# Rounding x for the last four row tiles on ScalarE: one step moved, and every engine's order written anew

## The reference, cut to what matters

```python
x = x + xattn(layernorm(x), ctx, ctx, mask, ...)      # 16 heads of 32; scores -> mask -> softmax -> v -> @ wo + bo
x = x + ffn(layernorm(x), w1, b1, w2, b2)

def act_quant(x):                                      # per row, to whole numbers from -127 to 127
    scale = 127.0 / clip(max(abs(x)), 1e-05)
    return clip(round(x * scale), -128, 127) / scale
def weight_quant(w):                                   # per matrix, to -1, 0, 1
    scale = 1.0 / clip(mean(abs(w)), 1e-05)
    return clip(round(w * scale), -1, 1) / scale
def bitlinear(x, w, b):
    return act_quant(rmsnorm(x)) @ weight_quant(w).T + b
h = gelu(bitlinear(x, w1, b1))                         # 512 -> 2048
return bitlinear(h, w2, b2)                            # 2048 -> 512
```

## Time and profile before

| | |
|---|---|
| median of 3 runs | 652.19 us (651.63 to 652.81) |
| the profiled execution | 650.6 us, span 648.8 us |
| granted TensorE clock | 1.000 in the mean, in every slice of the page |
| busy: PE / DVE / ACT / POOL | 628.9 / 574.3 / 530.2 / 518.7 us |
| share of the chain that ended last | PE 67%, POOL 13%, DVE 8%, DMA 4%, ACT 4%, issue 3% |

### The profile page before, as it was taken

One profiled execution on the slowest core, in us unless ns is written; L12 is line 12 of the kernel. 1 busy time (PEld: TensorE's weight loads), 2 busy tenths in 40 slices (PEclk: granted clock), 3 DMA queues, 4 the chain that ended last, 5 costly groups with the idle time before them and its releaser, 6 DMA issues.

```text
span 648.8 us, 14114 instructions
## 1 busy us (share of the span) xinstructions
PE 628.9 (97%) x4904; PEld 423.7 (65%) x4904; DVE 574.3 (89%) x1062; ACT 530.2 (82%) x1450; POOL 518.7 (80%) x653
## 2 busy tenths in 40 slices
PE   8988999999999999999999999999999999999996
PEld 6746886666666676766666676666667666565542
DVE  5697889999999988999899988999889799999894
ACT  2579679987889888887898878888988889998674
POOL 3297977979977898688967899778959778999776
PEclk9999999999999999999999999999999999999999
DMA  8983310424315443354224343043333122543236
GB/s 291 402 300 111 126 41 9 107 45 106 84 28 115 103 91 75 38 135 90 71 67 114 74 121 74 10 132 87 90 74 74 24 75 41 128 86 88 62 61 182
DMA packets 109286, 65.38 MB, mean 101 GB/s; under 512 B 90856, under 2 KB 90856, under 8 KB 108576
## 3 DMA queue, kind: packets, MB, share of 16 engines
q1 hardware_dynamic: 108159, 64.49, 37.9%
q10 hardware_dynamic: 1056, 0.00, 0.1%
HBM read 35.12 MB, written 8.39 MB: 67 GB/s over the span
## 4 chain that ended last, share of the span: by engine, by line
PE 67%; POOL 13%; DVE 8%; DMA 4%; ACT 4%; issue 3%; SPq 0%; POOLq 0%; DVEq 0%; ACTq 0%
PE ps_a L573 23%; PE ps_y L710 11%; PE ps_z L687 11%; PE ps_t L646 6%; PE ps_s L636 4%; PE ps_a L658 3%; POOL hid L2270 2%; POOL prob L2259 2%; DMA q_hT<-q_h 2%; PE ps_y L580 2%; DVE hs L1633 2%; POOL q_h L2275 2%; PE ps_a L607 2%; ACT prob L1145 2%; DMA wk_s<-in_L_xattn_wk_dram 1%
## 5 line engine op out<-in xcount | busy, mean ns | idle before, releaser
L1145 ACT ACTIVATE prob<-ps_s,nmax 128x120 f32<-128x120 f32 x512 | 178.9, 377 | 24.7 <-DVE nmax L1579 19.2
L2259 POOL TENSOR_TENSOR prob<-prob,pinv 128x480 f32<-128x480 f32 x128 | 129.2, 1017 | 41.0 <-DVE pinv L1584 40.0
L687 PE MATMUL ps_z<-w1T,q_xT 128*128 128x512 fp8e4 x476 | 122.8, 380 | 0.5 <-DVE hid L1625 0.4
L1145 ACT ACTIVATION_READ_ACCUMULATOR prob<-ps_s,nmax 128x1 f32 x512 | 113.3, 221 | 0.0
L710 PE MATMUL ps_y<-w2T,q_hT 128*128 128x512 fp8e4 x448 | 105.5, 379 | 1.5 <-DMA q_hT<-q_h 1.5
L1625 DVE SCALAR_TENSOR_TENSOR hid<-ps_z,y_deq,b_row 128x512 f32<-128x512 f32 x119 | 88.0, 739 | 10.6 <-PE ps_z L687 9.2
L1576 DVE COPY_PREDICATED_SCALAR ps_s<-hidden_key,masked_c 128x480 f32 x128 | 90.5, 707 | 4.2 <-PE ps_s L636 3.9
L1121 ACT COPY probT<-ps_t 120x512 f32<-120x512 f32 x128 | 76.9, 601 | 15.4 <-PE ps_t L646 14.3
L1579 DVE TENSOR_REDUCE nmax<-ps_s 128x4 f32<-128x480 f32 x128 | 84.1, 657 | 4.4
L646 PE MATMUL ps_t<-ident,prob 128*120 128x128 f32 x512 | 77.9, 275 | 4.3 <-POOL prob L2259 3.7
L646 PEld LDWEIGHTS ps_t<-ident,prob 128*120 128x120 f32 x512 | 60.0, 137 | 25.3 <-issue 7.4
(11 more groups left out here) (207 smaller groups left out, 1373.7 us busy)
## 6 DMA issues: line engine op xcount, KB each, us to landing
x<-in_x_dram SPq DMA_DIRECT2D x32, 256.0 KB, 2.9
out_dram<-x SPq DMA_DIRECT2D x32, 256.0 KB, 2.8
xn<-in_x_dram SPq DMA_DIRECT2D x7, 1024.0 KB, 6.6
hid<-in_L_ffn_w_dram SPq DMA_DIRECT2D x4, 1024.0 KB, 9.6
ctx_k<-in_ctx_dram SPq DMA_DIRECT2D x8, 240.0 KB, 3.1
ctx_k<-in_mask_Bx1xSxS_ik_dram SPq DMA_DIRECT2D x7, 240.0 KB, 3.1
xn<-in_x_dram SPq DMA_DIRECT2D x4, 256.0 KB, 3.5
x<-in_L_xattn_wq_dram SPq DMA_DIRECT2D x1, 1024.0 KB, 7.3
```

What stands on the lines that cost most here:

```text
L687: last = nc.tensor.matmul(bank[:], q_xT[:, k % 3, i], w1T[:, i, c * CH:(c + 1) * CH], start=(i == 0), stop=(i == KD - 1))
L1145: last = nc.scalar.activation(prob[:, n % 3, g * S2:(g + 1) * S2], ps_s[n % HG][:, g * S2:(g + 1) * S2], ACT.Exp, bias=nmax[:, n % 4, g:g ...
L2259: gp.tensor_tensor(pr, pr, pinv[:, n % 4].unsqueeze(2).to_broadcast([P, HG, S2]), ALU.mult).then_inc(s["prob_ready"], 1)
```

## The change

Two things change. For the row tiles 28 to 31 `round_x` on GpSimd ends after its first step, and a new `round_x` on ScalarE takes MAGIC off and writes q_x. And all five lists are written in another order; apart from the four new calls they hold the same calls as before. The parts of the diff that the prediction speaks of, from the lists with the unchanged lines left out:

```diff
+        XLATE = NT - 4
 # SP
-            load_piece(1)
-            load_piece(0)
-            load_piece(3)
-            load_piece(2)
+            load_piece(2)
+            load_piece(0)
+            load_piece(1)
+            load_piece(3)
...
 # TensorE, head
             turn_xn(0, 2)
+            turn_xn(0, 3)
             project_ctx(0, "k")
-            turn_xn(0, 3)
+            first_q(0)
             turn_keys(0)
-            first_q(0)
...
             turn_xn(1, 0)
-            turn_piece(3, (0, 1))
             turn_probs(2)
-            turn_piece(3, (2, 3))
+            turn_piece(3, (0, 1))
             turn_probs(3)
+            turn_piece(3, (2, 3))
             total_weights(1)
...
 # ScalarE
+            def round_x(k):
+
+                act.wait_ge(s["y_magic"], k + 1)
+                act.wait_ge(s[f"qxT{(k - 2) % 3}_in"], 16 * ((k - 2) // 3 + 1))
+                nc.scalar.activation(q_x[:, k % 2], yw[:, k % 2], ACT.Copy, bias=-MAGIC).then_inc(s["qx_ready"], 1)
+
...
 # VectorE, head: scale_bq() moves from before sum_abs(3) to behind weight_scales(0)
 # VectorE, tile 26
-            evac_up(27, 1)
             h_scale(26)
-            invert_sums(123)
             oT_low(29)
+            invert_sums(123)
             softmax_max(124)
...
 # GpSimd
             def round_x(k):
                 gp.tensor_scalar(yw[:, k % 2], yw[:, k % 2], yq[:, 2, t:t + 1], MAGIC, ALU.mult, ALU.add
                                  ).then_inc(s["y_magic"], 1)
+                if k >= XLATE:
+                    return
                 pool.wait_ge(s["y_magic"], k + 1)
...
             round_x(28)
             normalize(123)
+            add_bo(29)
             round_h(26)
             normalize(124)
-            add_b2(27)
+            add_b2(26)
             normalize(125)
...
 # GpSimd, before normalize(112): h_factor(23) and add_b2(25) move behind it
```

More of the change, by code:

```diff
@@ L451, in _ @@
             turn_x(3)
+            turn_h(1)
             load_mask(2)
-            turn_h(1)
+            turn_x(4)
             load_ctx(3)
@@ L878, in _ @@
             project_q(2, 2)
+            turn_probs(26)
+            ffn_up(3, 3)
             turn_ctx(3)
-            ffn_up(3, 3)
-            turn_probs(26)
             project_out(5)
@@ L1516, in _ @@
             gelu(29)
+            round_x(31)
             square_h(29)
@@ L2366, in _ @@
             y_factor(1)
-            add_bo(2)
-            normalize(15)
+            normalize(17)
             add_b2(1)
-            normalize(16)
-            normalize(17)
-            add_bo(3)
+            round_x(2)
+            normalize(18)
             add_bo(4)
-            round_x(2)
-            add_bo(5)
-            normalize(18)
-            y_factor(2)
-            normalize(19)
-            normalize(20)
-            round_h(0)
-            h_factor(0)
+            normalize(19)
@@ L2382, in _ @@
+            round_h(0)
+            normalize(20)
+            y_factor(2)
+            h_factor(0)
+            add_bo(5)
             add_b2(2)
-            y_factor(3)
             normalize(21)
             round_x(3)
+            y_factor(3)
+            add_b2(3)
             normalize(22)
-            add_b2(3)
             round_h(1)
             ln1_factors(3, 0, 4, 12)
+            ln1_apply((0, 1))
             normalize(23)
             normalize(24)
-            ln1_apply((0, 1))
             h_factor(1)
+            normalize(25)
@@ L2394, in _ @@
+            add_b2(4)
             round_x(4)
-            normalize(25)
+            ln1_apply((2, 3))
+            normalize(26)
             round_h(2)
-            normalize(26)
-            ln1_apply((2, 3))
+            normalize(27)
             y_factor(4)
-            normalize(27)
-            add_bo(6)
             normalize(28)
             h_factor(2)
+            add_bo(6)
             normalize(29)
             round_h(3)
-            add_b2(4)
             for a in range(2, 6):
+                round_x(4 * a - 3)
@@ L2409, in _ @@
                 y_factor(4 * a - 3)
-                round_x(4 * a - 3)
                 normalize(16 * a - 2)
+                normalize(16 * a - 1)
+                normalize(16 * a)
                 add_bo(4 * a - 1)
                 h_factor(4 * a - 5)
-                add_b2(4 * a - 3)
-                normalize(16 * a - 1)
-                normalize(16 * a)
                 round_x(4 * a - 2)
                 normalize(16 * a + 1)
+                round_h(4 * a - 4)
                 normalize(16 * a + 2)
+                h_factor(4 * a - 4)
@@ L2420, in _ @@
                 normalize(16 * a + 3)
+                normalize(16 * a + 4)
+                add_b2(4 * a - 3)
+                y_factor(4 * a - 2)
                 add_bo(4 * a)
-                round_h(4 * a - 4)
-                y_factor(4 * a - 2)
-                normalize(16 * a + 4)
                 normalize(16 * a + 5)
+                round_x(4 * a - 1)
+                normalize(16 * a + 6)
+                y_factor(4 * a - 1)
+                round_h(4 * a - 3)
+                normalize(16 * a + 7)
@@ L2437, in _ @@
-                ln1_factors(a + 2, 0, 4, 3 * a + 9)
-                normalize(16 * a + 10)
-                round_h(4 * a - 2)
                 add_b2(4 * a)
```

800 lines of the change are left out of this document (401 added, 399 removed).

## The result

| | before | after |
|---|---|---|
| median | 651.33 us (20 runs: 650.31 to 652.81, and one at 908.49) | 654.38 us (20 runs, 652.12 to 658.01) |
| ratio | | 1.0045, 95% interval 1.0032 to 1.0058 |
| profiled execution | 650.6, span 648.8 | 655.14, span 653.3 |

Slower by 0.45%, some 2.9 us, and with more scatter: eight of the twenty runs lie between 652.1 and 652.9, the other twelve between 653.1 and 658.0. I had 652.3 and 0.48 on no change; it came out on the side to which I gave 0.27, 0.08 above the end of my range (654.3, which was 2.1 above the median of before; measured are 3.05 above the median of twenty).

What follows compares the result with a forecast made beforehand. TensorE's own work bounds the loop, four engines bind one another from 535 to 603 us, and tile 29's q_h fixes the end. +1.05 - 0.60 - 0.39 + 0.1 = +0.16 on the 652.19 median: 652.3 us, range 650.3 to 654.3.

Steps and rivals of the forecast that it cites:

- rival 2: Head loss paid in full, nothing absorbed, through ScalarE's evacuations of weight piece 3: +1.75, 653.95 us; chance 0.22.
- The head, +1.05: Before the loop: later weight sum, GpSimd's and ScalarE's new orders delay the second weight-sum product; +1.05, bounds 0.25 and 1.65.
- my own point (57.1): In the head: a second line-719 product starting later than 57.1 us decides for the rival of a fully paid head.
- gave back 0.60: Late TensorE finds its awaited normalize ready at 102 us: 0.60 taken back, bounds 0 and 1.85.
- The middle: From 103 to 535 us: 0 for the loop itself, bound +1.8 for four passes of one wait.
- 535 to 603 us, -0.39 and +0.1: Normalize(112) freed of work ahead, -0.39; tile 26's q_h later through add_bo(29), +0.1, bounds -1.6 and +0.5.
- The moved step, 0 (bounds -0.3 to +0.6): Late tiles 28 to 31: four q_x roundings go from GpSimd to ScalarE as 0.60-us copies, hidden or without gain; 0.
- The tail, 0 (bounds -0.5 to +0.8): After 603 us: VectorE has the same work up to h_scale(29), so tile 29's q_h arrives as before; 0.
- Rival 1: End is won: GpSimd relieved, TensorE's waits of 0.38, 0.68 and 1.03 go; -1.64, 650.55 us; chance 0.20.
- Rival 3: Table changes: a switch takes 2.66 instead of 1.28, ScalarE late at 140 us; +2.8, 655.2 us; chance 0.03.
- Rival 4: round_x on GpSimd was covered anyway; all difference comes from the orders; no chance of its own.
- The signs: Profile after: line-719 products near 27.1 and 57.0, tile 26's wait under 1.6, last long wait for tile 29's q_h.

Runs made afterwards that it cites:

- a1: Kernel before with the five head lists of the kernel after, loops, tails and moved step as before: 1.0002, 651.55 us.
- a3: Kernel before with the loop lists of the kernel after, heads and tails as before: 1.0003 (0.9994 to 1.0012).
- a2: Kernel before with the five tail lists of the kernel after and the moved step, heads and loops as before: 1.0053, 654.72 us.
- b2: Kernel before with the tail lists of the kernel after, but round_x's second step kept on GpSimd for all tiles: 1.0041, 653.72 us.
- c1: Kernel after with GpSimd's add_bo(29) moved back behind normalize(120), no longer ahead of round_h(26): 1.0045, ten runs from 652.04 to 658.90 us.
- d2: Kernel after with SP's load_residual(28) moved behind turn_x(26), ahead of turn_h(24): 1.0022, 652.39 us.
- c2: Kernel after with VectorE's subtraction of the mean in the summing form for tile 30 alone: 1.0034, 653.29 us.
- a4: Kernel after with VectorE's subtraction of the mean in the summing form for all tiles: 1.0076, 656.52 us.
- b1: Kernel before, all its lists, with only round_x's second step of tiles 28 to 31 moved to ScalarE: 1.0073, 655.82 us.

## Why the prediction missed, step by step

The span of the profile after is 4.53 us longer than that of before. By the lags 0.2 of this were there at 454 us, where I had +0.45; 1.75 more came by gelu(27), where I had -0.29; 2.2 more up to the last half gelu and 0.4 behind it, where I had 0. So the steps that failed are the stretch from 535 to 603 us and the tail. That the median still lies close to the end of the range is owed to a width taken for other reasons: rival 2, in the head.

- **The head, +1.05.** The step was right inside the head: the second product of line 720 came 0.86 to 0.95 further behind the first (I had 0.8), through the order that I had listed (the last evacuation of ScalarE released it). By my own point (57.1) it even came on the side of rival 2, with 57.5. But I gave back 0.60, with waits I could see; measured is nearly all of it, by 116 us (a1, 0.1 left). The head was worth no term of the sum.
- **The middle.** The loop was worth nothing (a3), as taken, bound of 1.8 not needed.
- **535 to 603 us, -0.39 and +0.1.** Wrong in both. The wait for normalize(112) at 555 went, but the tail's lists put the softmax maxima 1.0 and 1.1 us behind by 575 (lags of a2 and b2, against those at 454). I foresaw add_bo(29) ahead of round_h(26); it took its 1.30. I missed that reciprocal(123) would come behind oT_low(29), at 590.51 and not at 589.08, and GpSimd's wait of 1.21 for the residual of tile 28, which SP's new list loads behind store(23): I had read SP's list only around the transposes of tile 28. And I missed three stalls: the subtractions of tiles 23 to 25 are 1.9 us longer in sum, on the engine that I had called full.
- **The moved step, 0 (bounds -0.3 to +0.6).** In the lists of this change the term holds as far as can be told: b2 and a2 differ by 0.8, intervals overlapping, and their profiles, less the lag, by nothing. The queue of SP that I named costs turn_h(26) 0.03. But the reasoning was thin, as the old lists show, where the same move costs 4.8. There store(24) stands behind turn_x(28), and I had followed no entry of the queue but the first, whose consumer, ffn_up of tile 28, comes late enough; turn_h(26) has a consumer that waits already. And "ScalarE has idle time" for tile 30 priced the copy, 0.60, which was measured 0.61 to 0.68, and not the wait (1.94 in the kernel after), nor square_h(28) behind it. That the new lists hide this was not in my sum.
- **The tail, 0 (bounds -0.5 to +0.8).** This is the largest miss: measured are 2.2 and 0.4. VectorE "has no idle time to lose" was blind to its durations: a stall that is recorded inside an instruction, 1.3 to 1.5 us at tile 30 and 0.5 at tile 31. And its one gap, 1.66 at 604.07 before, was no fixed thing: it grew to 1.92 with the late q_h of tile 26. The trace of before showed the stall, as 0.99 us at every fourth tile in place of 0.48 and as 0.68 at tile 30, and I had taken the mean of the line.
- **Rivals.** Rival 1 did not come. Rival 2 had the sign and the wrong place. Rival 3: two table loads more cost nothing (both are in the heads: a1 has 56 and the ratio 1.0002, a3 has 54 like before). A load and the next ACTIVATE of the kernel after:

```profile
468.22 1.28 ACT L1146 ACT_TABLE_LOAD   x1
469.51 0.36 ACT L1146 ACTIVATE prob<-ps_s,nmax 128x120 f32<-128x120 f32 x1
```

  By the rule that I weighed there (the Trainium skill, "ScalarE: Activation LUTs", section "What ACT_TABLE_LOAD costs"), a drain on top, the second would have stood at 470.9 by an estimate with its 2.66 us; it stands at 469.51. Rival 4, all from the orders, which my sum held too, is the one that fits: the new tails without the move have 1.0041 of the 1.0045 (b2). It does not hold in the old lists, where the move costs by itself.
- **The signs.** The head came as named, 27.3 and 57.5 on equal terms for 27.1 and 57.0, and tile 26's wait, 0.92, stayed under my 1.6. The sign that failed is TensorE's last long wait for q_h of tile 29, 14.4 us before the end: it is 0.52, not the longest, and behind it stands one of 0.37.

## What to carry to other kernels

A step moved to an idle engine must be priced with its wait, not its length: ask what stands behind it in that in-order list, and who waits for that. The price belongs to the lists around it: 4.8 us in the old ones here, nothing that could be told in the new. Do the same for every entry of the DMA queue behind the first that slips, down to the one whose consumer is already waiting. And read the longest instance of each instruction, not the mean, since an engine can stall inside an instruction that no idle time shows. Last, look at the clock of every run before explaining scatter by the program.

## What the runs showed of the hardware

- A VectorE subtraction, SBUF to SBUF in float32 with one tensor input, did not run beside a GpSimd instruction that had started first: 0.48 us alone, 0.99 at every fourth tile of before, 1.20 beside an add_bo of 1.28 (tile 24 of the kernel after), 1.99 beside the 1.90 of round_h(27), ending 0.3 after it. Where the subtraction started first, it took 0.49 and GpSimd's step 2.11 in place of 1.90 (c1, d2). The form that also sums takes 0.74 in either case. The Trainium skill, "SBUF — State Buffer", section "Who interferes with whom", says that a tensor_scalar in a two-port mode and GpSimd exclude each other for a whole instruction, and excepts the summing form; the traces agree in the exclusion and in the exception, with these numbers; that the plain form runs in such a mode no run here shows by itself.
- After a wait of 2.21 us on TensorE the granted clock fell to 1.2 GHz for about 3 us and cost 1.7 (c2); it fell likewise after waits of 1.96 (a4) and, in the head, 1.97 (a1). It is no rule: b1's profile has a wait of 2.50 at 603.84 and a clock of 1.00 in every stretch behind it.
